# Rotating raw query and key projections out of PSUM, dividing by their norms afterwards, with a new order over a pair of tiles

## The reference, cut to what matters

```python
q, k, v = split(shift_tokens(x) @ Wqkv)           # 16 heads of 64 each
q = l2norm(q) * q_scale;  k = l2norm(k) * k_scale # over the 64 of a head
q = q * cos * scale + rotate_half(q) * sin * scale
k = k * cos / scale + rotate_half(k) * sin / scale
out = local_attention(q, k, v)                    # windows of 32, own and previous
x = out @ Wo + x
x = ffn_layer(shift_tokens(x)) + x                # layer norm, gated GELU, two products
```

## Time and profile before

| what | number |
|---|---|
| median of 3 runs (lowest, highest) | 2010.42 us (2004.8, 2011.33) |
| span of the profiled execution, first to last instruction | 2010.7 us |
| TensorE matmul busy | 1805.9 us, 90% |
| VectorE busy | 1557.0 us, 77% |
| GpSimd busy | 1455.2 us, 72% |
| ScalarE busy | 1164.3 us, 58% |

### The profile page before, as it was taken

One profiled execution on the slowest core, in us unless ns is written; L12 is line 12 of the kernel. 1 busy time (PEld: TensorE's weight loads), 2 busy tenths in 40 slices (PEclk: granted clock), 3 DMA queues, 4 the chain that ended last, 5 costly groups with the idle time before them and its releaser, 6 DMA issues. The chain is left out here.

```text
span 2010.7 us, 85596 instructions
## 1 busy us (share of the span) xinstructions
PE 1805.9 (90%) x34280; PEld 1311.9 (65%) x34280; DVE 1557.0 (77%) x2776; ACT 1164.3 (58%) x1966; POOL 1455.2 (72%) x967
## 2 busy tenths in 40 slices
PE   7774689999999999999999999999999999999995
PEld 3453466676776666766666666667676667676764
DVE  4764688887888878888788788887887888878864
ACT  2311356666666666666666666666666666666662
POOL 3221688877887778777877787778777877787771
PEclk9875899999999999999999999999999999999997
DMA  4000122223222223222223322233222232222220
GB/s 151 2 3 1 44 65 65 59 54 86 73 70 53 55 63 91 59 70 63 61 53 84 77 68 55 52 82 81 63 58 59 63 86 63 70 63 55 55 58 22
DMA packets 93581, 123.43 MB, mean 61 GB/s; under 512 B 27760, under 2 KB 41808, under 8 KB 93392
## 3 DMA queue, kind: packets, MB, share of 16 engines
q1 hardware_dynamic: 93232, 122.42, 24.2%
q10 hardware_dynamic: 288, 0.13, 0.0%
HBM read 20.74 MB, written 1.05 MB: 11 GB/s over the span
## 5 line engine op out<-in xcount | busy, mean ns | idle before, releaser
L999 POOL TENSOR_TENSOR across<-unit,turns 128x1024 f32<-128x1024 f32 x192 | 497.4, 2591 | 279.7 <-issue 268.4
L1006 POOL TENSOR_TENSOR rotated<-along,across 128x1024 f32<-128x1024 f32 x192 | 496.7, 2587 | 14.2
L1151 DVE TENSOR_REDUCE sums<-squares 128x16 f32<-128x1024 f32 x192 | 234.2, 1220 | 173.2 <-ACT squares L1054 173.1
L1247 PE MATMUL turn<-identity,rotated 128*128 128x128 f32 x1536 | 205.2, 277 | 36.4 <-POOL rotated L1006 36.4
L1247 PEld LDWEIGHTS turn<-identity,rotated 128*128 128x128 f32 x1536 | 172.6, 141 | 98.9 <-issue 83.4
L1032 POOL TENSOR_TENSOR along<-unit,turns 128x1024 f32<-128x1024 f32 x96 | 228.3, 2378 | 0.0
L1352 PE MATMUL proj_a<-w_qkv,shift_a 128*128 128x512 f32 x384 | 189.9, 617 | 36.4 <-DVE unit L1176 30.1
L1113 ACT COPY val<-proj_a 128x1024 f32<-128x1024 f32 x96 | 97.2, 1013 | 181.3 <-PE proj_a L1352 181.3
L1377 PEld LDWEIGHTS att<-o_t,w_o 128*128 128x128 f32 x1536 | 188.0, 193 | 6.1 <-issue 1.0
L1377 PE MATMUL att<-o_t,w_o 128*128 128x128 f32 x1536 | 188.3, 276 | 0.0
L1280 PE MATMUL proj_a<-w_qkv,shift_a 128*128 128x512 f32 x384 | 183.5, 601 | 4.3 <-POOL shift_a L988 3.0
(11 more groups left out here) (203 smaller groups left out, 3445.2 us busy)
## 6 DMA issues: line engine op xcount, KB each, us to landing
v_win<-val SPq DMA_DIRECT2D x1536, 64.0 KB, 2.0
w_qkv<-wqkv_dram SPq DMA_DIRECT2D x18, 512.0 KB, 3.8
w_o<-wo_dram SPq DMA_DIRECT2D x6, 512.0 KB, 4.6
where<-positions_dram SPq DMA_DIRECT2D x1, 2048.0 KB, 11.4
w_ffn<-ffn_dram SPq DMA_DIRECT2D x12, 170.5 KB, 2.3
w_ffn<-ffn_dram SPq DMA_DIRECT2D x6, 192.0 KB, 2.3
x_tok<-x_dram SPq DMA_DIRECT2D x4, 256.0 KB, 4.3
out_dram<-final SPq DMA_DIRECT2D x4, 256.0 KB, 2.4
```

The source lines that it names most:

```text
L999: pool.tensor_tensor(a[:, :, ::-1, :], u, table, ALU.mult).then_inc(acrossed[j], 1)
L1006: pool.tensor_tensor(rotated[j][:, :, :], along[j][:, :, :], across[j][:, :, :], ALU.add).then_inc(rotated_in[j], 1)
L1151: dve.tensor_reduce(sums[:, j, :], squares[j][:, :, :], AX.X, ALU.add).then_inc(summed[j], 1)
L1247: mm = pe.transpose(bank[:, TILE * (i % 4):TILE * (i % 4) + TILE], buffer[:, TILE * i:TILE * i + TILE], identity[:, :])
```

## The change

The rotation is now made on VectorE straight out of PSUM: `turn_raw` writes `along` and `across` from the raw projection and the tables, for queries and keys alike (four products of 128 x 1024 a tile). `unite` and the buffer `unit` are gone. GpSimd adds the two (`add_turned`, into `rotated`, which now has two buffers for each of queries and keys), and once the root is there multiplies the sum by the inverse norm in place (`divide`). GpSimd's `across` and `along` are gone. The value projection waits for `across` of the queries instead of `unite`, and the next key projection for `across` of the keys.

The step is now one pair of tiles, `step(u)` with u = pair, and each engine's order is written out anew over the pair; a loop of 42 rounds runs it. The widening product of pair u - 2 stands in one piece ahead of the first key projection of the pair. The mask products, all matrix products and all ScalarE operations are the same in number and shape. On SP, the loads of `w_o` and of the up weights move one value spread later.

```diff
-        inv_norm = sb("inv_norm", [128, 2, HEADS])
+        inv_norm = [sb(f"inv_norm{i}", [128, 2, HEADS]) for i in range(2)]
-        unit = [sb(f"unit{i}", [128, HEADS, HEAD]) for i in range(2)]
-        rotated = [sb(f"rotated{i}", [128, HEADS, HEAD]) for i in range(2)]
+        rotated = [[sb(f"rotated{j}{i}", [128, HEADS, HEAD]) for i in range(2)] for j in range(2)]
...
-                    pool.wait_ge(united[j], p + 1)
-                    pool.tensor_tensor(a[:, :, ::-1, :], u, table, ALU.mult).then_inc(acrossed[j], 1)
...
+                def divide(j, n, odd):
+                    pool.wait_ge(added[j], n + 1)
+                    pool.wait_ge(rooted, ROOT_OPS * n + ROOT_OPS)
+                    pool.tensor_tensor(rotated[j][odd][:, :, :], rotated[j][odd][:, :, :],
+                                       inv_norm[odd][:, j, :].unsqueeze(2).broadcast_to([128, HEADS, HEAD]),
+                                       ALU.mult).then_inc(rotated_in[j], 1)
...
+                def turn_raw(j, n, odd):
+                    raw, table = (bank_a, bank_b)[j], turns[odd]
+                    dve.wait_ge(squared[j], n + 1)
+                    dve.wait_ge(table_made, n + 1)
+                    after(dve, added[j], n)
+                    dve.tensor_tensor(along[j][:, :, :], by_head(raw),
+                                      table[:, 2 * j, :].unsqueeze(1).broadcast_to([128, HEADS, HEAD]),
+                                      ALU.mult).then_inc(alonged[j], 1)
+                    dve.tensor_tensor(halves(across[j][:, :, :])[:, :, ::-1, :], halves(by_head(raw)),
+                                      table[:, 2 * j + 1, :].rearrange("p (two e) -> p two e", two=2).unsqueeze(1)
+                                      .broadcast_to([128, HEADS, 2, HEAD // 2]), ALU.mult).then_inc(acrossed[j], 1)
...
+                def project_values(n, odd):
+                    pe.wait_ge(acrossed[0], n + 1)
...
+                    if has(u + 1):
+                        if has(u - 2):
+                            pe.wait_ge(gated, NC_ * (u - 1) - 1)
+                            stand_alone(pe, passed)
+                        project_keys(u * 2 + 2, 0)
```

More of the change, by code:

```diff
@@ L901, in layers @@
         XA_BASE = 8
-        FIRST, ROUNDS = 7, 44
+        DUOS = STEPS // 2
+        FIRST, LAST = 4, DUOS - 2
         def by_head(bank):
@@ L907, in halves, with has, tiles_to @@
         def halves(buffer):
-            return buffer[:, :, :].rearrange("p h (two e) -> p h two e", two=2)
+            return buffer.rearrange("p h (two e) -> p h two e", two=2)
         def up_out(i):
             return (bank_b[:, 0, :], bank_b[:, 1, :], bank_t[:, 1, :])[i]
[L913 to L917, removed]
-        def run(engine, step):
[L922 to L928, removed]
+        def has(duo):
+            return not isinstance(duo, int) or 0 <= duo < DUOS
+        def tiles_to(n):
+            return min(n, STEPS) if isinstance(n, int) else n
+        def run(engine, step):
+            for u in range(-2, FIRST):
+                step(u)
+            with engine.Fori(0, LAST - FIRST) as i:
+                step(i + FIRST)
+            for u in range(LAST, DUOS + 2):
+                step(u)
         with nc.Block() as block:
@@ L1001, in add_turned @@
[L1001 to L1042, removed]
@@ new lines, in square, with keep_probs @@
+                def square(j, n):
+                    act.wait_ge((q_projected, k_projected)[j], n + 1)
+                    after(act, summed[j], n)
+                    act.activation(squares[j][:, :, :], by_head((bank_a, bank_b)[j]), ACT.Square).then_inc(squared[j], 1)
+                def keep_probs(n):
+                    for j in range(2):
+                        act.wait_ge(p_turned, 2 * n + j + 1)
+                        after(act, mixed, 2 * n)
+                        act.copy(p_t[:, 4 * j:4 * j + 4, :], bank_s[:, j, :].rearrange("p (a t) -> p a t", t=TILE))\
+                            .then_inc(p_laid, 1)
@@ new lines, in sum_squares, with root @@
+                def sum_squares(j, n):
+                    dve.wait_ge(squared[j], n + 1)
+                    after(dve, rooted, ROOT_OPS * n)
+                    dve.tensor_reduce(sums[:, j, :], squares[j][:, :, :], AX.X, ALU.add).then_inc(summed[j], 1)
+                def root(n, odd):
+                    dve.wait_ge(summed[0], n + 1)
+                    dve.wait_ge(summed[1], n + 1)
+                    after(dve, rotated_in[0], n - 1)
+                    after(dve, rotated_in[1], n - 1)
+                    inverse_root(dve, range(ROOT_OPS), sums[:, :, :], sums_min[:, :, :], inv_norm[odd][:, :, :],
+                                 [w[:, :, :] for w in root_work], magic[:, :, :], rooted, ROOT_OPS * n)
@@ new lines, in project_keys @@
+                def project_keys(n, odd):
+                    pe.wait_ge(k_in, (layer_of(n) + 1) * 16)
+                    after(pe, acrossed[1], n)
+                    stand_alone(pe, passed)
+                    for half in range(2):
+                        base = INNER + 512 * half
+                        mm = pe.matmul(bank_b[:, half, :], shift_a[odd][:, :], w_qkv[:, base:base + 512],
+                                       start=True, stop=True)
+                    mm.then_inc(k_projected, 1)
```

720 lines of the change are left out of this document (410 added, 310 removed).

## The result

The changed kernel takes 1924.62 us (median of 4 runs, 1921.36 to 1933.09) against 2010.88 us for the kernel before (median of 4 runs): ratio 0.9585, 95% interval 0.956 to 0.9609. The forecast was 1935 us in a range of 1905 to 1985. The profiled span fell by 87.7 us, from 2010.7 to 1923.0 us.

What follows compares the result with a forecast made beforehand. TensorE was taken to bound the layers; 34.42 + 0.28 + 0.30 = 35.0 us a pair saves 67.5 us over 45 pairs, and filling 8 us: 2010.7 - 67.5 - 8 = 1935 us, range 1905 to 1985.

Steps and rivals of the forecast that it cites:

- 2.07 us of idle time a pair: Sum of TensorE's timeline waits per pair of tiles: 0.50, 0.45, 0.25, 0.59 and 0.28 us; all there is to win.
- The floor: TensorE's time for a pair without idle time: 36.49 - 2.07 = 34.42 us, taken as unchanged by the change.
- The loop edge: TensorE's 0.28 us wait put down to issue at the loop body's first instruction; was to stay, ahead of a query projection.
- The two tight places: First key projection of a pair and turning of the even tile's keys: 0.3 us a pair together, bounds 0 and 1.3.
- The five waits: TensorE's waits for divided heads, unite (two value projections), rotated keys and issue; all but issue's 0.28 us were to go.
- the key projection behind the gate: Pair's first key projection, waiting until VectorE gated two chunks: 8.7 us against 8.62 of cover, a tenth of a microsecond short.
- Filling: Start of the kernel, up to tile 4: 8 us of gain, bounds 0 and 13.
- The drain: End of the kernel, the last pair's norm and block: same chain as before, no difference taken.
- (a): Rival: waits move rather than go, the tight places costing half a microsecond or more at both tiles; 1980 us, chance 0.18.
- (b): Rival: the order gives nothing, equally long waits elsewhere; 36.3 to 36.5 us a pair, about 2000 to 2010 us, chance 0.05.
- (c): Rival: GpSimd's sums hold up VectorE's root, its first operation waiting up to 2.2 us; slower, 2093 us, chance 0.09.

Runs made afterwards that it cites:

- the doubled weight sum: The changed kernel with VectorE's sum of the even tile's weights made twice, just ahead of the gating: 1973.53 us, ratio 0.9828.
- the first two experiments: Kernel before with the new rotation where unite stood: 2136.59 us; the same with raw products ahead of the root, old order of steps: 2476.87 us.

## Why the prediction was right

**The bound.** It held that TensorE bounds the layers and that its 2.07 us of idle time a pair is all there is to win. The pair gave back 36.50 - 34.24 = 2.26 us, more than that sum, and taking the mask products off gave 1.0 us more: TensorE still bounds, now together with VectorE's chain through the gate.

**The pair, 35.0 us forecast, 34.24 measured.** The term was too high in three places. The floor: 34.42 was the old pair less its idle time, but TensorE's busy time a pair is now 358.02 / 360 x 34.24 = 34.05 us, 0.37 less. In part the rows show why: next to a wait TensorE's distances are longer by more than the bracket. In the kernel before:

```profile
1041.51 1.09 PE L1247 MATMUL turn<-identity,rotated 128*128 128x128 f32 x8
1043.11 1.09 PE L1247 MATMUL att<-identity,heads_out 128*128 128x128 f32 x8 [0.51 <-DVE heads_out L1157]
```

Without the bracket that is 1.60 - 0.51 = 1.09 us; turned keys without a wait behind them take 0.93 now (1021.03 to 1021.96). So the busy time of the pair held some of the waits' cost, and taking it for a floor was the step that was too high; the whole 0.37 is not accounted for. The loop edge: 0.28 was to stay and is gone (1025.62 to 1026.55 is 0.93 us, as from 1010.77 to 1011.70 at the other tile, which has no edge); what takes it away is not shown. The two tight places: 0.30 forecast, 0.19 left, at the first key projection; the turned keys of the even tile show none. 0.37 + 0.28 + 0.11 = 0.76 us, 34 us over 45 pairs.

**The five waits** went as reasoned, and what became late next was the key projection behind the gate, as named; the doubled weight sum shows that it has no slack.

**Costs.** Raw products 1.21 us (1.22 taken). By the Trainium skill ("SBUF — State Buffer", section "Who interferes with whom") two SBUF inputs contend with GpSimd's reads and one does not; the trace agrees on both sides, 1.21 us from PSUM and 2.35 for `along` from SBUF. VectorE 30.5 us a pair (30.9). GpSimd 20.9 (23): the division takes 1.90 us, under the lower bound of 2.35, which rested on another operation of the same shape.

**The ends.** Filling gained 6.9 us (8). The drain (tile 94 to the end) lost 9.2 where nothing was put, and the first four pairs behind tile 4 lost 11 over the steady pace: this term was not in the sum. The experiments tie the loss behind tile 4 to the code written out ahead of the loop, which costs nothing in the order of before; for the drain only the pauses point there. The errors partly cancel: -34 for the pair, +11 and +9 at the ends, +1 in the fill, in all 12 us under the sum. That the sum came so near is in part luck.

**The rivals.** (a) and (b) fell: no wait took the place of the old ones. (c) did not happen in the loop: the root's first operation is 0.30 us at one tile, beside an input copy, where 2.1 was the price of a catch. That price was right when forced. At the even tile's root such a catch is absorbed; at the odd tile's, ahead of the gate, the doubled weight sum lets expect that it would come through nearly in full, which was not tested. That the change is two changes which need each other, the prediction did not ask; the first two experiments show one side of it, that the rotation needs the order.

## What to carry to other kernels

Where one engine is busy 94% of a stretch, add up the waits that its timeline names: that sum is about the gain to be had (2.07 us named, 2.26 gained here), and a change is worth what it takes from it. A buffer should be released by work that does not need the late scalar, and the scalar applied afterwards where there is room; but move the rest of the queue along with it, or the operations that are pushed back cost more than the wait. Once an engine has no waits left, look at the code written out around the loop: what bringing it in costs, hidden before, can show.

## What was not expected of the hardware

- TensorE pauses of up to 2.9 us inside a run of 128 small products, only while the instruction queue moves packets of 16 KB (0.92 MB / 56); 2.9 us a written-out pair here, none in the loop. The Trainium skill ("Runtime: NRT & Kernel Launch", section "Instruction fetch mechanics") has code streamed in blocks of 16 KiB by a queue of its own, which agrees, and mostly hidden, which the order of before agrees with and the new one does not.
- GpSimd's in-place product with a broadcast operand takes 1.90 us, a sum of two full operands of the same size 2.37.
- With waits of 4 us at every tile TensorE's granted clock went to 0.50 at each and was 0.88 in the mean from 900 to 1260 us; with waits of up to 1.3 us (the rotation alone, order of before) it was 1.00 in the same stretch.
